# Layer 1 of a two-layer graph network: from lane-wise running sums to sorted edge tiles, node blocks and accumulating gathers

## The reference, cut to what matters

```python
# layer 1, on x that layer 0 left; edges: edge_attr_32 (E x 32), W1: 160 x 128, W2: 128 x 64
concat = [x[src], x[dst], edges]                     # E x 160
h = relu(concat @ W1 + b1)                           # E x 128
messages = h @ W2 + b2                               # E x 64
aggregated = segment_sum(messages, dst) / max(degree, 1)
x = layernorm(x + aggregated + x @ Wn + bn)          # N x 64
```

## Time and profile before

| | us |
|---|---|
| median of three runs (5617.39 to 5643.6) | 5635.98 |
| the profiled execution, from its first to its last instruction (its span) | 4755.7 |
| the median less that span | 880.3 |
| POOL busy in the span | 3565.7 |
| DVE busy | 2619.7 |
| PE busy | 1308.6 |
| ACT busy | 493.5 |

### The profile page before, as it was taken

One profiled execution on the slowest core, in us unless ns is written; L12 is line 12 of the kernel. 1 busy time (PEld: TensorE's weight loads), 2 busy tenths in 40 slices (PEclk: granted clock), 3 DMA queues, 4 the chain that ended last, 5 costly groups with the idle time before them and its releaser, 6 DMA issues. The chain is left out here.

```text
span 4755.7 us, 33914 instructions
## 1 busy us (share of the span) xinstructions
PE 1308.6 (28%) x3363; PEld 660.9 (14%) x3363; DVE 2619.7 (55%) x8568; ACT 493.5 (10%) x1011; POOL 3565.7 (75%) x3558
## 2 busy tenths in 40 slices
PE   7600000000000000000575333333333333333336
PEld 4300000000000000000453111111111111111126
DVE  6545443344433444433774666666666666666645
ACT  4500000000000000000232111111111111111101
POOL 5777777777777777777676777777777777777766
PEclk9855555555555555555555655655665556556655
DMA  3034333333333333333232555555555555555532
GB/s 124 10 112 160 100 105 118 118 117 112 93 118 118 118 118 99 106 118 113 85 121 94 169 171 167 165 170 170 162 170 171 161 170 171 166 166 171 170 104 63
DMA packets 240932, 622.28 MB, mean 131 GB/s; under 512 B 74956, under 2 KB 102543, under 8 KB 221521
## 3 DMA queue, kind: packets, MB, share of 16 engines
q1 hardware_dynamic: 127568, 443.81, 28.2%
q0 software_dynamic: 113280, 177.74, 14.7%
HBM read 328.11 MB, written 293.29 MB: 131 GB/s over the span
## 5 line engine op out<-in xcount | busy, mean ns | idle before, releaser
L525 POOL DMA_INDIRECT edge_arena<-table1s,ix x1568 | 1518.0, 968 | 477.9 <-issue 435.2
L433 POOL DMA_INDIRECT edge_arena<-table,ix x1440 | 1460.5, 1014 | 438.9 <-issue 438.9
L565 PE MATMUL ps<-w1e_bd,edge_terms 128*128 128x512 f32 x784 | 725.1, 1080 | 1264.4 <-DMA edge_terms<-e32g_d 1264.4
L1191 DVE SCALAR_TENSOR_TENSOR edge_arena<-edge_arena,same 128x128 f32<-128x128 f32 x1568 | 542.0, 346 | 263.6 <-issue 189.1
L565 PE MATMUL ps<-we_bd,edge_terms 128*128 128x32 f32 x392 | 93.6, 403 | 1864.1 <-DVE score L1038 1803.8
L1035 DVE TENSOR_TENSOR score<-edge_arena,node_wide 128x128 f32<-128x128 f32 x49 | 14.2, 291 | 1066.0 <-DMA edge_arena<-table,ix 1065.6
L1057 DVE TENSOR_TENSOR_SCAN edge_arena<-wq,edge_arena 128x32 f32<-128x32 f32 x3136 | 586.8, 268 | 1.8
L1197 DVE SCALAR_TENSOR_TENSOR edge_arena<-edge_arena,same 128x128 f32<-128x128 f32 x1568 | 539.7, 344 | 1.5 <-ACT edge_arena L832 1.2
L565 PEld LDWEIGHTS ps<-w1e_bd,edge_terms 128*128 128x128 f32 x784 | 229.0, 322 | 1759.2 <-issue 1759.2
L1209 DVE TENSOR_TENSOR edge_arena<-edge_arena 128x1024 f32<-128x1024 f32 x196 | 240.9, 1229 | 404.5 <-DMA edge_arena<-table1s,ix 404.5
L832 ACT ACTIVATE edge_arena<-edge_arena 128x1024 f32<-128x1024 f32 x196 | 207.0, 1056 | 1800.9 <-DVE edge_arena L1214 1800.9
(11 more groups left out here) (177 smaller groups left out, 1462.5 us busy)
## 6 DMA issues: line engine op xcount, KB each, us to landing
recv_term<-zeros SPq DMA_DIRECT2D x98, 1024.0 KB, 9.1
edge_arena<-recv_term SPq DMA_DIRECT2D x196, 512.0 KB, 4.1
rows<-edge_arena SPq DMA_DIRECT2D x196, 512.0 KB, 5.1
rows<-edge_arena SPq DMA_DIRECT2D x49, 1152.0 KB, 4.4
edge_arena<-table,ix POOLq DMA_INDIRECT x1568
edge_terms<-e32g_d SPq DMA_DIRECT2D x196, 128.0 KB, 4.8
edge_arena<-table1s,ix POOLq DMA_INDIRECT x1568
edge_terms<-e16g_d SPq DMA_DIRECT2D x49, 256.0 KB, 9.2
```

The lines of the kernel that those rows point to most:

```text
L433: pool.indirect_dma_start(G0[slot][:, u, :], None, table0, bass.IndirectOffsetOnAxis(ap=ix[slot][:, u:u + 1], axis=0)).then_inc(gathered0[ ...
L525: pool.indirect_dma_start(G1[slot][:, u, :], None, table1s, bass.IndirectOffsetOnAxis(ap=ix[slot][:, u:u + 1], axis=0)).then_inc(gathered1 ...
L565: return pe.matmul(out_, lhsT, rhs, start=start, stop=stop)
L1191: stt(X[:, u, :], X[:, u - 1, :] if u else Xb[:, C1 - 1, :], same[:, bass.ds(c * C1 + u, 1)], X[:, u, :], ALU.mult, ALU.add).then_inc(dv1, 1)
```

## The change

Layer 1 no longer works along lanes. The edges, in their sorted order, form `T` = 1563 tiles of 128 edges; four tiles are a group (391 groups), two groups a chunk (196 chunks). The nodes form 98 blocks of 128. A step (there are 391 + 97 = 488) is one group against one of the blocks that its edges' receivers fall in.

- **Edge term ahead of time.** During layer 0, `edge_term` on PE makes the edge term of each chunk (8 matmuls of 128 x 512), `edge_out` on ACT evicts it and stores it to `terms1` in HBM (196 DMAs of 512 KB on ACT's queue). The clearing of `recv_term` is gone.
- **Preparation in the middle of layer 0**, after chunk 24: DVE and PE build from `dst` the table of steps (block, group, ring slot, last chunk needed), `local` (each edge's receiver within the block) and `keep`, and turn `src` into tile order.
- **Node stage:** `scatter_first` is gone. SP sends `src` and the step table through HBM before the first node chunk.
- **Start of layer 1:** the receiver rows of all blocks are loaded into SBUF (`Rj`), DVE adds `b2` in 100 instructions of 64 columns, the result is stored to `rows_own`, and only then SP loads the first edge rows.
- **Layer 1:** SP loads a chunk's rows of `terms1` into the ring `G1` (8 slots); when they have landed, POOL's gathers of `table1s` add to them (`compute_op=ALU.add`). For each step DVE makes the one-hot matrix edge x node (`hot`), PE transposes it and multiplies it by the block's receiver rows (`pre`), DVE adds that to the ring's rows (`hidden`), ACT casts, copies and applies relu, PE multiplies by the one-hot matrix to sum by node (`aggregate`), DVE adds the sum to the block's place in `RA` (`gather_up`, which overwrites the receiver rows). PE, DVE and SP read the step's block, slot and counts from the table into registers with `TENSOR_LOAD`.
- **End:** 98 matmuls by `W2` in 14 batches of 7 blocks, layer norm and store. No gathers.

The diff, cut to its core:

```diff
 RING0 = 4
 G0E = P // F16
-C1 = 8
-K1 = LANE // C1
-RING1 = 4
+T = (E + P - 1) // P
+GT = 4
+GE = GT * P
+GROUPS = (T + GT - 1) // GT
+NJ = (N + P) // P
+STEPS = GROUPS + NJ - 1
+SPAN = 512
+TC = SPAN // P
+CHUNK = 2
+CHUNKS = (GROUPS + CHUNK - 1) // CHUNK
+RINGC = 8
+RINGG = RINGC * CHUNK
+AHEAD = 4
+BLK = 7
...
-                for z in range(2):
-                    sp.dma_start(recv_flat[:, bass.ds(c * (2 * ZERO_COLS) + z * ZERO_COLS, ZERO_COLS)],
-                                 zeros[:, :]).then_inc(recv_zeroed, 16)
                 sp.wait_ge(edge_mm, c + 1)
                 if not (isinstance(c, int) and c + 2 >= K0):
                     sp.dma_start(edge_terms[par][:, :, :], e16g[:, bass.ds(c * 4 + 8, 4), :]).then_inc(e16_in[par], 16)
+                if not (isinstance(c, int) and c + 1 >= K0):
+                    for half in range(2):
+                        sp.wait_ge(term_mm, c * TG + (half + 1) * TG // 2)
+                        sp.dma_start(edge_terms[2 + half][:, :, :],
+                                     e32g[:, bass.ds(c * TG + (TG + half * TG // 2), TG // 2), :]).then_inc(e32_raw[half], 16)
                 sp.wait_ge(rows0_ready, c + 2)
                 sp.dma_start(rows0_p[:, bass.ds(c * C0, C0), :], R0[par]).then_inc(rows0_stored[par], 16)
...
+            sp.wait_ge(src_ready, 1)
+            sp.dma_start(src_d, src_by_tile[:, 0:TILES]).then_inc(src_stored, 16)
+            sp.wait_ge(src_stored, 16)
+            sp.dma_start(src_t[:, :], src_d).then_inc(src1_in, 16)
+            sp.wait_ge(tabs_ready, 1)
+            sp.dma_start(steps_d, steps_new.rearrange("p k c -> p (k c)")).then_inc(steps_stored, 16)
+            sp.wait_ge(steps_stored, 16)
+            sp.dma_start(steps_i, steps_d).then_inc(steps_in, 16)
...
+                sp.wait_ge(pds_stored[r], 16 * (NK // 2 + 1))
+                sp.wait_ge(term_stored[r], 16 * (2 * K0 + 1))
+            sp.dma_start(Rj.rearrange("p (j f) -> p j f", f=HID), block_rows(table1d[0:NJ * P, :])).then_inc(R_in, 16)
+            sp.wait_ge(own_ready, 1)
+            sp.dma_start(rows_own_q, node_wide[:, :]).then_inc(own_stored, 16)
+            sp.wait_ge(own_stored, 16)
+            for c in range(AHEAD):
+                edges(c, c)
+            for c in range(2):
+                sp.wait_ge(e32_in[c], 16)
+                sp.sem_inc(e_landed, 1)
+
...
+            def chunk1(slot, it, c, ended, tiles=CHUNK * GT, load=True, more=True):
+
+                if ended is not None:
+                    sp.reg_alu(sp_due, ended, 1, ALU.max)
+                    sp.wait_ge(h_ready, sp_due)
+                if load:
+                    edges(c + AHEAD, (slot + AHEAD) % RINGC)
+                if more:
+                    sp.wait_ge(e32_in[(slot + 2) % RINGC], it * 16 + ((slot + 2) // RINGC * 16 + 16))
+                    sp.sem_inc(e_landed, 1)
+                sp.wait_ge(gathered1[slot], it * (16 * CHUNK * GT) + 16 * tiles)
+                sp.sem_inc(landed, 1)
...
-            def scatter_first(r):
-                for b in range(NC):
-                    pool.indirect_dma_start(recv_term, bass.IndirectOffsetOnAxis(ap=start_ix[r][:, b:b + 1], axis=0),
-                                            PDs[r][:, b, :], None, bounds_check=NE - 1, oob_is_err=False).then_inc(pds_scattered[r], 16)
-
...
+            pool.wait_ge(src1_in, 16)
+            for t in range(T):
+                c, u = divmod(t, CHUNK * GT)
+                if u == 0:
+                    pool.wait_ge(e_landed, c + 1)
+                pool.indirect_dma_start(G1[:, t % (RINGG * GT) * HID:t % (RINGG * GT) * HID + HID], None, table1s,
+                                        bass.IndirectOffsetOnAxis(ap=src_t[:, t:t + 1], axis=0), compute_op=ALU.add).then_inc(gathered1[c % RINGC], 16)
...
+            def edge_term(c, it):
+                for m in range(TG):
+                    if m % (TG // 2) == 0:
+                        pe.wait_ge(e32_raw[2 * m // TG], c * 16 + 16)
+                    pe.wait_ge(term_used, c * TG + (m + 1))
+                    mm(ps[:, 6 + m % 2, :], edge_terms[2 + 2 * m // TG][:, m % (TG // 2), :], w1e_bd[:, :]).then_inc(term_mm, 1)
...
+            def turned(k, i):
+
+                pe.wait_ge(hot_ready, k + 1)
+                if not (isinstance(k, int) and k < 2):
+                    pe.wait_ge(A_ready, k - 1)
+                for u in range(GT):
+                    last = pe.transpose(turned_ps[i % 2][:, u * P:(u + 1) * P], B16[i % 4][:, u, :], ident16[:, :])
+                last.then_inc(turned_mm, 1)
+
+            def pre(k, i, row):
+
+                j = row[0]
+                bank = ps[:, 2 + i % 2, :]
+                if not (isinstance(k, int) and k < 2):
+                    pe.wait_ge(h_ready, k - 1)
+                pe.wait_ge(A_ready, k + 1)
+                for u in range(GT):
+                    last = mm(bank[:, u * HID:(u + 1) * HID], A32[i % 2][:, u * P:(u + 1) * P], Rj[:, bass.ds(j, HID)])
+                last.then_inc(pre_mm, 1)
+
+            def aggregate(k, i):
+
+                pe.wait_ge(relu_done, k + 1)
+                pe.wait_ge(cast_ready, k + 1)
+                if not (isinstance(k, int) and k < 4):
+                    pe.wait_ge(agg_done, k - 3)
+                for u in range(GT):
+                    last = mm(ps[:, 4 + i % 4, 0:P], H1[i % 4][:, u * HID:(u + 1) * HID], B32[i % 4][:, u, :], u == 0, u == GT - 1)
                 last.then_inc(agg_mm, 1)
...
+            def edge_out(c):
+                for m in range(TG):
+                    q, half = divmod(m, 2)
+                    act.wait_ge(term_mm, c * TG + (m + 1))
+                    if half == 0:
+                        act.wait_ge(term_stored[q % 2], c * 32 + (q // 2 * 16 + 16))
+                    act.activation(stage[q % 2][:, half * GE:(half + 1) * GE], ps[:, 6 + m % 2, :], ACT.Copy).then_inc(term_used, 1)
+                    if half:
+                        act.wait_ge(term_used, c * TG + (m + 3))
+                        act.dma_start(terms1_p[:, bass.ds(c * (C0 * HID) + q * 2 * GE, 2 * GE)], stage[q % 2]).then_inc(term_stored[q % 2], 16)
...
+            def ahead(k, i):
+
+                act.wait_ge(turned_mm, k + 1)
+                if not (isinstance(k, int) and k < 2):
+                    act.wait_ge(pre_mm, k - 1)
+                act.activation(A32[i % 2], ps[:, i % 2, 0:GE // 2].bitcast(BF16), ACT.Copy).then_inc(A_ready, 1)
+                act.wait_ge(hot_ready, k + 1)
+                if not (isinstance(k, int) and k < 4):
+                    act.wait_ge(agg_mm, k - 3)
+                act.activation(B32[i % 4][:, :, :], B16[i % 4][:, :, :], ACT.Copy).then_inc(cast_ready, 1)
+
+            def relu(k, i):
+
+                act.wait_ge(h_ready, k + 1)
+                act.activation(H1[i % 4], H1[i % 4], ACT.Relu).then_inc(relu_done, 1)
...
+            for b in range(NB):
+                last = stt(own[:, b, :], row_bc[:, 2, :], has[:, b:b + 1], own[:, b, :], ALU.mult, ALU.add)
+            last.then_inc(own_ready, 1)
...
+            def hot(k, i):
+
+                if not (isinstance(k, int) and k < 4):
+                    dve.wait_ge(turned_mm, k - 3)
+                    dve.wait_ge(cast_ready, k - 3)
+                tt(B16[i % 4][:, :, :], hot_iota, wide(local[:, bass.ds(k * GT, GT)].unsqueeze(2), [P, GT, P]), ALU.is_equal).then_inc(hot_ready, 1)
+
+            dve_due = dve.alloc_register("dve_due")
+
+            def hidden(k, i, row):
+
+                _, _, g, landed_by = row
+                dve.reg_alu(dve_due, landed_by, 1, ALU.max)
+                dve.wait_ge(landed, dve_due)
+                dve.wait_ge(pre_mm, k + 1)
+                if not (isinstance(k, int) and k < 4):
+                    dve.wait_ge(agg_mm, k - 3)
+                tt(H1[i % 4], G1[:, bass.ds(g, GE)], ps[:, 2 + i % 2, :], ALU.add).then_inc(h_ready, 1)
+
+            def gather_up(k, i, row):
+
+                j = row[0]
                 dve.wait_ge(agg_mm, k + 1)
...
+                    dve.wait_ge(agg_done, k)
+                state = RA[:, bass.ds(j, HID)]
+                stt(state, state, keep[:, bass.ds(k, 1)], ps[:, 4 + i % 4, 0:P], ALU.mult, ALU.add).then_inc(agg_done, 1)
```

641 lines of the change are left out of this document (372 added, 269 removed).

## The result

The kernel after took 5989.75 us (median of four runs, 5987.0 to 5995.2), the kernel before 5639.02 beside it: a ratio of 1.066, 95% interval 1.062 to 1.069. It is slower, as forecast, but by 6.6% and not by 1.8%.

What follows compares the result with a forecast made beforehand. POOL's gather pitch was taken as the bound. Terms of 5 - 13 + 17 + 14 - 91 = -68 us, plus 172 for accumulation, gave +104: 5740 us, 1.8% over the median; range 5545 to 6100 us.

Steps and rivals of the forecast that it cites:

- The bound: Both edge stages: POOL issues gathers at a pitch of 1.249 us without waiting for anybody, so its instructions set the span.
- The accumulation: Layer 1 gathers: adding to the destination costs POOL 0.11 us more each, +172 us over 1563 (0 to +907).
- The upper bound: Layer 1 gathers: accumulating costs at most a second DMA of 128 descriptors, 0.58 us each, +907 us in all.
- break-even of 0.044 us: Layer 1 gathers: extra POOL time per accumulating gather at which the whole change neither wins nor loses, 68 / 1563.
- Rival B: Layer 1: accumulation is dear (descriptors written twice), or DMA engines or register loads set the loop; from 5960 us; chance 0.18.
- rival A: Layer 1 gathers: accumulation costs POOL nothing, time 5568 us, faster than before; chance 0.30.
- The 880 us: Outside the profiled span: 880.3 us between span and median time, kept unchanged because inputs and output are the same.
- Layer 0: Layer 0: edge-term work hidden behind gathers at 0, preparation holding up POOL for moments; +5 us (0 to 20).
- Node stage and start of layer 1: Between the layers: no scatters, -13 us; a new chain of additions, store and load before the first gather, +17 us.
- Hold-up by `hot`: Layer 1: gathers starting within this two-input SBUF instruction wait, 0.12 us per step, 57 us (0 to 268).
- Other engines in the loop: Layer 1 steps: DVE, ACT, PE, register loads and DMA engines fit under POOL's pitch, costed at nothing.
- The end: After the last gather: 80 us in place of 171, without running-sum gathers; -91 us (-105 to -70).

Runs made afterwards that it cites:

- f1_after: The kernel after, unchanged, profiled in a short session: 5584.8 us against 4756.6 for the kernel before, ratio 1.174.
- g2_plain: The kernel after with plain layer 1 gathers that overwrite the loaded edge rows, in a long session: 5840.2 us against 5621.7 for the kernel before.
- g3_pe_term: The kernel after with plain gathers, no layer 0 edge term, PE making it in layer 1; long session: 5847.8 us, 1.041 of the kernel before.
- f4_plain: The kernel after with plain layer 1 gathers that overwrite the loaded edge rows, in a short session: 4710.3 us.
- e3_old_acc: The kernel before with its 1568 layer 1 gathers adding to stale ring rows instead of overwriting them, in a short session: 5824.9 us against 4765.2.

## Why the prediction missed

**The bound was read rightly for the profile at hand.** POOL's pitch sets layer 1 of the kernel after, and anything that lengthens one of 1563 gathers shows 1563 times. In the profile after, they stand without another wait ahead of them than "issue", but for the first, as the prediction asked. The kernel before has the same bound in the short kind only.

**The accumulation was mis-sized, and this is the step that failed first.** Forecast 0.11 us a gather, +172 us; measured 0.600 us between the medians, 938 us, of which the shorter hold-up gives 60 back: 876 us of layer 1 (2908.8 less 2032.5). The value was four times the extra cost of a bounds check. The upper bound, a second DMA of 128 descriptors for the 0.58 us of the earlier trace rows, came nearest, and the truth lies slightly above it. Two ends 0 and 907 us apart, and I went to the cheap one because the scatter was "nearest"; but a scatter with a check is the same kind of instruction, while none of the trace reads its destination. The break-even of 0.044 us said that only a nearly free accumulation wins; with ends like these the expensive end needed more than 0.18. Rival B names the mechanism, a dear instruction on POOL; whether its reason, descriptors written twice, is the true one no run shows, and the price for each row (1.3 ns more) is not what carries it. Its second reason, the DMA engines, falls: from 3000 to 4000 us of f1_after they are busy for 0.42 of the time, with plain gathers for 0.36.

The Trainium skill (DMA: Bandwidth & Descriptors, Anatomy of one DMA — SWDGE (gpsimd) path) says that many descriptors can be emitted before the incremental cost shows. For the rows of one gather the trace agrees in part: 64 rows more cost 0.045 us plain and 0.129 us accumulating. The rule does not speak of what the change adds, and taken as rival A it failed.

**The 880 us were no constant around the span, and the engines beside POOL were not free.** The prediction kept the 880 us and named it as a root error if they should change, and it put the other engines at nothing (layer 0's new work "at a cost of 0", the loop's with POOL's pitch as cover). This is the second step that failed. The 880 us lie within the span in the long kind, and there the terms of the sum are others: DVE's gaps cost the kernel before 530 us in layer 1, and without any accumulation the change still costs 202 us where -68 was forecast. Layer 1 of the kernel after is 2908 us long in either kind, since its slow gathers cover the gaps. So the accumulation's price is 876 us of layer 1 in the short kind and 197 in the long one. That the 5990 us lie inside the range (5545 to 6100) is luck, and so is it that the 172 us forecast for the accumulation are near its worth in the long kind (some 150 us of span): in the kind whose profile I read, the change costs 830 us and not 104.

The other terms, against the short kind:

- *Layer 0*: +5 forecast, +9 measured. The matmuls, evictions and stores of the edge term are covered; the version without them ends it at 2261.8, 3.3 us earlier. In the long kind they are not: with them it ends at 2634.6 (g2_plain), without them at 2511.1 (g3_pe_term) in the same session. The groups above show where: POOL's idle time ahead of line 559 is 756 us instead of 439, 324.6 of it for DVE's line 1225. There is no result for the kernel after with nothing but this work left out (e4_no_terms), so the two versions compared differ in layer 1 as well.
- *Node stage and start of layer 1*: -13 and +17 forecast. In the short profile after, the last table is stored at 2558.53, 5.5 us earlier than the earlier trace rows although layer 0 ended 8.5 later: -14. The chunk's period is 23.9 us (24.2 forecast), taken at line 1377, the same addition as line 1148 in the earlier trace rows. (The first period there is 23.2 us, not the 23.1 of the prediction.) From that store to the first gather it is 41.0 us, where 43 were forecast (+15 instead of +17): the `b2` additions took 19.7 instead of 25, store and landing the rest. The first gather stands at 2599.6; I had named 2599. The timeline of f1_after:

```profile
2558.53 0.33 SPq L438 DMA_DIRECT2D table1d<-node_arena  x1
2559.31 19.67 DVE L1400 SCALAR_TENSOR_TENSOR node_wide<-row_bc,has,node_wide 128x64 f32<-128x64 f32 x100 [19.09 <-DMA table1s<-node_arena]
2561.68 0.87 SPq L463 DMA_DIRECT2D node_arena<-table1d  x1
2579.01 3.88 SPq L465 DMA_DIRECT2D rows_own<-node_wide  x1
2594.53 4.03 SPq L457 DMA_DIRECT2D edge_arena<-terms  x4
2599.57 1.58 POOL L637 DMA_INDIRECT edge_arena<-table1s,src_idx  x1 [111.20 <-SPq L471]
```

- *Hold-up by `hot`*: 57 us forecast. With plain gathers the mean is 996 ns over a median of 947: 77 us. With accumulating ones it is 1558 over 1547: 17 us, because only 82 of the gathers of f1_after start while a `hot` runs, against 298 of those of f4_plain. Starts at random would give about 266 and 180 (0.68 us of `hot` over a pitch of 1.25 and of 1.85 us), so beside the accumulating gathers they do not fall at random. Two moments of f4_plain, in its timeline:

```profile
3503.24 0.69 DVE L1411 TENSOR_TENSOR same<-iota_k,zeros 128x512 bf16<-128x512 f32 x1
3503.28 1.47 POOL L637 DMA_INDIRECT edge_arena<-table1s,src_idx  x1 [0.30 <-issue]
...
3504.70 0.68 DVE L1411 TENSOR_TENSOR same<-iota_k,zeros 128x512 bf16<-128x512 f32 x1
3505.05 1.15 POOL L637 DMA_INDIRECT edge_arena<-table1s,src_idx  x1 [0.30 <-issue]
```

A plain gather that starts within `hot` typically ends 0.82 us after it, as in the earlier trace rows; an accumulating one ends 1.42 us after it, as beside line 1209 in e3_old_acc. The inference of the Trainium skill (SBUF — State Buffer, Who interferes with whom) that `tensor_tensor` does not stall a software DMA does not hold for this form; the price was right in kind, a quarter too low for plain gathers and three times too high for the accumulating ones.
- *Other engines in the loop*: nothing forecast, nothing found in the short kind; for the long kind see above. The loads of the step table into registers, for which no row stood, take 1.13 us (PE), 1.6 us (DVE) and 0.58 us (SP) at the median in the records of f1_after, once for four steps on PE and DVE.
- *The end*: 80 us forecast, 74.7 measured.

Without the accumulation I had summed -68 us; the kernel with plain gathers comes out at -44 in the short kind. The 24 us are layer 1 (+26, of them 20 the hold-up), layer 0 (+5), the way between them (-1) and the end (-6).

## What to carry to other kernels

A gather that adds to its destination is not a gather with the addition thrown in: it cost POOL 1.547 us instead of 0.947, with rows of 256 bytes as with 512. Where POOL sets the pace, the sum belongs on an engine with room: in the short kind PE made it and the kernel took 4708 us instead of 5585. If no row of the trace shows an operation, the two bounds are the forecast, and a value at the cheap end needs a reason of its own. When the times and the profile's span disagree by 16%, find out first which of them is the machine that will be measured: a change is worth something else where another engine is the pace, and a term put at nothing because another engine covers it has to be asked again.

## What the runs showed that I had not expected

- The same kernel before took 4757 or 5632 us by session. In the long kind DVE's scans stand 0.70 or 1.40 us apart for stretches, instead of 0.186, and single register steps of ACT and SP take 0.70 us; POOL's gathers keep their pitch of 1.249 us. By this the ratio of after to before went from 1.174 to between 1.05 and 1.07, and that of the version with PE's edge term from 0.988 to between 1.026 and 1.041. Its cause was not found.
- A plain gather of 128 rows makes 16 packets of data and one of 64 rows makes 16 too; an accumulating one makes a packet for each row.
- POOL's price for a gather has little to do with rows: 0.902 us for 64 and 0.947 for 128 plain, 1.417 and 1.546 accumulating, and nothing to do with width (256 and 512 bytes tried, accumulating).
- How much a DVE instruction holds up POOL depends on when the two start: in two kernels that differ in the accumulation alone, `hot` caught 298 plain gathers and 82 accumulating ones.
